# A selective-scan kernel: a third product buffer, an earlier gate copy, and u's projection and the front spread over a batch's blocks in another way

## What is computed

```python
x = einsum('ed,bld->bel', in_proj_w, hidden_states)            # 1024 channels
xc = causal depthwise convolution of x, 4 taps
u = silu(xc + conv_b)
x_dbl = einsum('ke,bel->bkl', x_proj_w, u)                     # dt (32), B (16), C (16)
delta = softplus(dt_proj_w @ dt_lo + dt_proj_b);  A = -exp(A_log)
state = state * exp(d_t * A) + (d_t * u_t) * B_t               # 16 states for each channel
y_t = sum over n of state * C_t
y = (y + D * u) * silu(z)                                      # z = layernorm(x)
x = x + y
n = layernorm(x)
x = x + n @ W_base.T + b_base + top-2-gated low-rank experts of n
```

## Time and profile before

| | us |
|---|---|
| median of 3 runs | 2175.45 |
| lowest and highest | 2169.37, 2175.68 |
| profiled execution | 2179.93 |
| its span in the trace | 2178.1 |
| before the first scan | 91.1 |
| E0 to E31, from first scan to last scan's end | 1910.2 |
| behind the last scan | 176.8 |

### The profile page before, as it was taken

The page is one execution under the profiler, slowest core; times in us unless marked ns, Lnnn a source line. Parts: engine busy times, 40 slices in busy tenths (PEclk is TensorE's granted clock), DMA queues, the critical chain, the costliest instruction groups (busy, mean ns, idle before and its releaser), DMA issues.

```text
span 2178.1 us, 23728 instructions
## 1 busy us (share of the span) xinstructions
PE 1812.5 (83%) x7992; PEld 1097.9 (50%) x7992; DVE 1789.7 (82%) x1430; ACT 1255.9 (58%) x1701; POOL 1774.2 (81%) x798
## 2 busy tenths in 40 slices
PE   9877777777778888888888888888888888878999
PEld 3344444454455555555555555555555545555554
DVE  3589898888898899987999999987999999997111
ACT  3355555456566666655766666655766666663432
POOL 0389888889898998988999998988999999997300
PEclk9777787778779999998999999998999999999999
DMA  4665555576755656685666665685755556665300
GB/s 157 242 233 189 188 180 185 180 247 245 236 189 183 208 205 210 224 282 212 221 207 210 214 206 205 222 277 176 240 195 202 201 205 213 213 213 193 136 29 34
DMA packets 157977, 435.88 MB, mean 200 GB/s; under 512 B 14528, under 2 KB 47552, under 8 KB 157728
## 3 DMA queue, kind: packets, MB, share of 16 engines
q1 hardware_dynamic: 157856, 434.37, 58.1%
HBM read 383.46 MB, written 50.86 MB: 199 GB/s over the span
## 4 chain that ended last, share of the span: by engine, by line
DVE 33%; PE 30%; POOL 15%; issue 13%; ACT 6%; DMA 4%; SPq 0%; DVEq 0%; POOLq 0%; ACTq 0%
DVE state L1051 21%; POOL prod L1188 10%; DVE row L1036 9%; PE bank_a L548 7%; PE y_ps L492 6%; POOL drive_rows L1181 3%; PE bank_b L443 3%; DVE conv L1028 3%; PE bank_b L548 3%; PE row L570 3%; DMA xrow<-in_x 2%; ACT decay L807 2%; PE bank_b L472 2%; PE row L486 1%; PE bank_b L452 1%
## 5 line engine op out<-in xcount | busy, mean ns | idle before, releaser
L1188 POOL TENSOR_TENSOR prod<-state,c_rows 128x1024 f32<-128x1024 f32 x512 | 1201.2, 2359 | 163.4 <-PE y_ps L492 132.9
L1051 DVE TENSOR_TENSOR_SCAN state<-decay,row 128x1024 f32<-128x1024 f32 x332 | 758.0, 2283 | 9.5 <-POOL prod L1188 2.4
L492 PEld LDWEIGHTS y_ps<-ident,prod 128*128 128x128 f32 x4096 | 516.7, 152 | 343.3 <-issue 173.9
L492 PE MATMUL y_ps<-ident,prod 128*128 128x128 f32 x4096 | 596.9, 294 | 82.8 <-POOL prod L1188 81.2
L1036 DVE TENSOR_TENSOR row<-du,row 128x1024 f32<-128x1024 f32 x332 | 402.1, 1211 | 105.5 <-PE row L486 102.9
L1051 DVE TENSOR_TENSOR_SCAN state<-row,drive_rows 128x1024 f32<-128x1024 f32 x180 | 409.8, 2277 | 21.8 <-POOL drive_rows L1181 21.5
L1181 POOL TENSOR_TENSOR drive_rows<-du,b_rows 128x1024 f32<-128x1024 f32 x180 | 425.4, 2364 | 2.0 <-DMA b_rows<-bc_d 2.0
L807 ACT ACTIVATE row<-delta,a 128x1024 f32<-128x1024 f32 x180 | 201.0, 1117 | 389.2 <-DVE state L1051 388.8
L548 PE MATMUL bank_a<-w_o,xnT 128*128 128x512 f32 x816 | 400.2, 622 | 30.1 <-DVE x L1098 30.1
L807 ACT ACTIVATE decay<-delta,a 128x1024 f32<-128x1024 f32 x332 | 372.2, 1135 | 0.1
L486 PE MATMUL row<-parts,sel 96*128 96x512 bf16 x664 | 221.7, 418 | 119.4 <-DVE state L1051 114.4
(11 more groups left out here) (131 smaller groups left out, 1653.1 us busy)
## 6 DMA issues: line engine op xcount, KB each, us to landing
c_rows<-bc_d SPq DMA_DIRECT2D x512, 512.0 KB, 4.3
xrow<-in_x SPq DMA_DIRECT2D x32, 512.0 KB, 6.6
skip<-u_d SPq DMA_DIRECT2D x32, 512.0 KB, 5.8
yy_d<-yy SPq DMA_DIRECT2D x32, 512.0 KB, 6.2
b_rows<-bc_d SPq DMA_DIRECT2D x24, 512.0 KB, 6.0
u_d<-conv SPq DMA_DIRECT2D x24, 512.0 KB, 5.3
ctx<-u_d SPq DMA_DIRECT2D x48, 256.0 KB, 5.9
x<-in_x SPq DMA_DIRECT2D x24, 512.0 KB, 5.9
```

The costliest lines, as they stand in the source:

```text
L492: last = nc.tensor.matmul(y_ps[:, i * P:(i + 1) * P], source[:, i * P:(i + 1) * P], ident[:, :], start=(first and i % (H // P) == 0), stop ...
L1051: nc.vector.tensor_tensor_scan(state[:, q % STATES, :], factor, term, 0.0, ALU.mult, ALU.add).then_inc(scan_done, 1)
L1188: nc.gpsimd.tensor_tensor(prod[:, q % PRODS, :], state[:, q % STATES, :], c_rows[:, q % RING, :], ALU.mult).then_inc(prod_ready, 1)
```

## The change

PRODS goes from 2 to 3 and RING from 5 to 4, the same memory. The front's table has one form for all batches: blocks 0 to 5 of a batch make 3, 3, 2, 3, 3, 2 halves of the next batch and blocks 6 and 7 none (before, batches 1 and 2 had 3, 2, 2, 3, 2, 2, 0 and block 7 began the batch after next with two). Where it is spread out, the first half's pieces move from sections 0 to 3 to sections 2, 3, 4, 4, and its conv and taps from 5 to 6. turn_gate stands in sections 2 and 3 and take_gate in 3 and 4, but in a batch's last block in 4, 5 and 5, 6. reduce_u of the first half is in sections 5 to 8 of block 6, two matmuls each, and that of the second half in sections 0 to 3 of block 7; the copies, the split, dt_half, the gate's sums, store_bc, load_b, load_us and load_ctx move behind it. The diff:

```diff
--- before.py
+++ after.py
@@ -24,7 +24,7 @@
 LATE = 9
 FIRST_SPLITS = 6
 FIRST_TAIL = NBLK - LATE
-RING, DECAYS, STATES, PRODS, DRIVES = 5, 4, 3, 2, 2
+RING, DECAYS, STATES, PRODS, DRIVES = 4, 4, 3, 3, 2
 
 
 
@@ -32,19 +32,15 @@
 DECAY_AT[12] = DECAY_AT[13] = 10
 
 
-EARLY = [[(0, 0), (0, 1), (1, 0)], [(1, 1), (2, 0), (2, 1)], [(3, 0), (3, 1)], [(4, 0), (4, 1), (5, 0)],
+FRONT = [[(0, 0), (0, 1), (1, 0)], [(1, 1), (2, 0), (2, 1)], [(3, 0), (3, 1)], [(4, 0), (4, 1), (5, 0)],
          [(5, 1), (6, 0), (6, 1)], [(7, 0), (7, 1)], [], []]
-LATER = [[(1, 0), (1, 1), (2, 0)], [(2, 1), (3, 0)], [(3, 1), (4, 0)], [(4, 1), (5, 0), (5, 1)],
-         [(6, 0), (6, 1)], [(7, 0), (7, 1)], [], [(0, 0), (0, 1)]]
 
 
 def front_halves():
     table = []
     for E in range(NBLK):
         b, r = E // NE, E % NE
-        ahead = b + (2 if r == NE - 1 else 1)
-        rows = EARLY if b == 0 and r < NE - 1 else LATER
-        table.append([(ahead * NE + c, h) for c, h in rows[r]] if ahead < B else [])
+        table.append([((b + 1) * NE + c, h) for c, h in FRONT[r]] if b + 1 < B else [])
     return table
 
 
@@ -52,7 +48,7 @@
 HALF_INDEX = {u: i for i, u in enumerate(u for row in HALVES for u in row)}
 
 
-SPREAD_OUT = (((0, 1, 2, 3), (5, 6, 7, 8), (9, 10, 11, 12)), (5, 10, 14), (5, 10, 15))
+SPREAD_OUT = (((2, 3, 4, 4), (5, 6, 7, 8), (9, 10, 11, 12)), (6, 10, 14), (6, 10, 15))
 IN_ONE_GO = (((5,), (8,), (12,)), (7, 10, 14), (7, 10, 15))
 
 
@@ -353,10 +349,11 @@
                 load_c(E * DS + m + RING - 1)
                 last = r == NE - 1 and b + 1 < B
                 if last:
-                    if m == 0:
+                    if m == 4:
                         store_bc(b + 1)
-                    if m - 1 in B_ROWS:
-                        load_b(b + 1, B_ROWS.index(m - 1))
+                    for i, n in enumerate(B_ROWS):
+                        if m == max(n + 1, 6 + i):
+                            load_b(b + 1, i)
                 if m == 2 and j >= 1:
                     store_half(j - 1, 1)
                 if m == 3:
@@ -382,10 +379,10 @@
                     if m == 0:
                         for s in range(NE):
                             load_us(b + 1, s)
-                    if m in (6, 7, 8):
-                        for s in range(NE + 3 * (m - 6), min(NE + 3 * (m - 6) + 3, 2 * NE)):
+                    if 7 <= m <= 10:
+                        for s in range(NE + 2 * (m - 7), NE + 2 * (m - 7) + 2):
                             load_us(b + 1, s)
-                if r == NE - 1 and m == 0 and b + 2 < B:
+                if r == NE - 1 and m == 5 and b + 2 < B:
                     for k in range(NK):
                         load_ctx(b + 2, k)
                 if E == NBLK - 1 and m == 6:
@@ -602,10 +599,17 @@
                 if ((q + 1) // DS, (q + 1) % DS) in D_INDEX:
                     spread((q + 1) // DS, (q + 1) % DS)
 
-                if m < 2 and E + 1 < NBLK:
+                last = r == NE - 1 and b + 1 < B
+                if last and m < 4:
+                    reduce_u(b + 1, 1, range(2 * m, 2 * m + 2))
+                if last and m in (4, 5):
+                    turn_gate(E, m - 4)
+                if last and m in (6, 7):
+                    dt_half(E + 1, m - 6)
+                if not last and m < 2 and E + 1 < NBLK:
                     dt_half(E + 1, m)
-                if m in (2, 4):
-                    turn_gate(E, m // 2 - 1)
+                if not last and m in (2, 3):
+                    turn_gate(E, m - 2)
 
                 if dense and m in (2, 3):
                     turn(j, m - 2, beside, True)
@@ -616,9 +620,9 @@
 
                 for i, at in enumerate(front_plan(E)[0]):
                     if m in at and len(HALVES[E]) > i and m < 9:
-                        project(E, i, [at.index(m)] if len(at) > 1 else range(NK))
-                if r == NE - 2 and b + 1 < B and 5 <= m <= 7:
-                    reduce_u(b + 1, 0, range(3 * (m - 5), min(3 * (m - 5) + 3, NE)))
+                        project(E, i, [k for k in range(NK) if at[k % len(at)] == m])
+                if r == NE - 2 and b + 1 < B and 5 <= m <= 8:
+                    reduce_u(b + 1, 0, range(2 * (m - 5), 2 * (m - 5) + 2))
 
                 if dense:
                     if m in (6, 7, 9, 10):
@@ -630,9 +634,7 @@
                         experts(j, 0, beside)
                 for i, at in enumerate(front_plan(E)[0]):
                     if m in at and len(HALVES[E]) > i and m >= 9:
-                        project(E, i, [at.index(m)] if len(at) > 1 else range(NK))
-                if r == NE - 2 and b + 1 < B and 12 <= m <= 14:
-                    reduce_u(b + 1, 1, range(3 * (m - 12), min(3 * (m - 12) + 3, NE)))
+                        project(E, i, [k for k in range(NK) if at[k % len(at)] == m])
                 if dense:
                     if m >= 13:
                         product(j, 1, range(3 * (m - 13), min(3 * (m - 13) + 3, NE)), beside, True)
@@ -919,35 +921,37 @@
                         make_decay(*step)
                 if m == 0:
                     scale_skip(E)
-                if m in (1, 2) and E + 1 < NBLK:
+                last = r == NE - 1 and b + 1 < B
+                if not last and m in (1, 2) and E + 1 < NBLK:
                     take_v(E + 1, m - 1)
+                if last and m == 4:
+                    take_xd(b + 1, 1)
+                    split_first(b + 1)
                 if dense and m in (3, 4):
                     take_turned(j, m - 3, beside, True)
-                if m in (3, 5):
-                    take_gate(E, (m - 3) // 2)
+                if not last and m in (3, 4):
+                    take_gate(E, m - 3)
+                if last and m in (5, 6):
+                    take_gate(E, m - 5)
+                if last and m in (7, 8):
+                    take_v(E + 1, m - 7)
+                if last and m == 7:
+                    split_second(b + 1)
                 if dense and m == 5:
                     take_routing(j, beside)
                 if dense and m == 7:
                     exp_gap(j)
                 if E + 1 < NBLK:
-                    if m == 7:
+                    if m == (8 if last else 7):
                         gate_sum(E + 1)
-                    if m == 8:
+                    if m == (9 if last else 8):
                         gate_squares(E + 1)
                     if m == 9:
                         gate_scale(E + 1)
-                if r == NE - 2 and b + 1 < B:
-                    if m == 8:
-                        take_xd(b + 1, 0)
-                    if m == 15:
-                        take_xd(b + 1, 1)
-                if r == NE - 1 and b + 1 < B:
-                    if m == 0:
-                        split_first(b + 1)
-                    if m == 3:
-                        split_second(b + 1)
-                    if m == 6:
-                        split_third(b + 1)
+                if r == NE - 2 and b + 1 < B and m == 9:
+                    take_xd(b + 1, 0)
+                if last and m == 10:
+                    split_third(b + 1)
 
                 if E + 1 < NBLK:
                     if m == 10:
@@ -1136,6 +1140,8 @@
                         dve.wait_ge(xd_copied, 2 * (b + 1) + 1)
                     elif len(HALVES[E]) > 1:
                         dve.wait_ge(conv_done, HALF_INDEX[HALVES[E][1]] + 1)
+                    elif r == NE - 1 and b + 1 < B:
+                        dve.wait_ge(v_copied, 2 * (E + 1))
                     else:
                         dve.wait_ge(gate_copied, 2 * E + 2)
                     gates(j, beside)
@@ -1218,8 +1224,8 @@
                 product(E * DS + m)
                 if j >= -1 and m in (7, 10):
                     add_x(j + 1, (7, 10).index(m))
-                if r == NE - 1 and b + 1 < B and m in (1, 4):
-                    split_rest_of(b + 1, m == 1)
+                if r == NE - 1 and b + 1 < B and m in (6, 8):
+                    split_rest_of(b + 1, m == 6)
                 if m == 12 and E + 1 < NBLK:
                     make_du(E + 1)
```

## The result

| | before | after |
|---|---|---|
| median, us | 2175.56 | 2099.48 |
| lowest and highest | 2169.37, 2183.69 | 2095.79, 2104.84 |
| profiled execution | 2179.93 | 2104.84 |
| before the first scan | 91.1 | 92.6 |
| blocks E0 to E31 | 1910.2 | 1835.7 |

A forecast was written before the change was run, and what follows sets the result against it. No engine is full; TensorE, working in order, hands its waits on to VectorE and GpSimd. Terms summed to -66.1 us, giving 2113.8 from the profiled execution, 2109 as median; range 2080 to 2150 us.

The forecast's parts named there:

- gate and third halves, E9 to E13, E16 to E21: Dense blocks: 16 us gained by copying the gate earlier, 5 us lost to third halves in four blocks.
- E14, E22: Block 6 of two batches: moving eight matmuls out takes each from 68.2 to 57.7 us, 21 us together.
- the gate's 1.6 us in ten blocks: Ten dense blocks: copying the gate a section earlier removes TensorE's bank wait, 16 us in all.
- the start's 3.4 us: First block: c row 3 now stands behind w_o's 4 MB load, so product 4 starts 3.4 us later.
- rival C: Crowded sections 3 to 5: c rows land late and GpSimd waits, 96 us slower, 2205 us; chance 0.07.
- Rival A: TensorE itself is the bound, so only moved matmuls and third halves count: 20 us gained, 2155 us; chance 0.16.
- the third product buffer: Product q waits for add-up q-3; worth lies in other parts and in batch 3, where 5 us were taken.
- the pieces of sections 0 to 2: Six spread-out blocks: moving two project pieces to sections 2 to 4 gains 3.5 us a block, 21 us.
- the third halves (+5 us in the sum): Blocks 1 and 4 of batches 1 and 2: an extra half each costs 9 us on VectorE, gives 4 back.
- the 2.7 us of idle time that I gave it from E19: First batch's block 7: GpSimd's work plus this idle time makes 57.5 us against 61.2, a gain of 3.7 us.
- the 2.9 us that the prediction added to E14 and E22: Sections 12 to 14 lose their filling, so TensorE's clock drops as in E10: 2.9 us a block.
- the split of x_dbl: Block 7, moved to sections 4 to 10: ScalarE's wait there was taken as 0, bounds 0 and 5 us.

The follow-up runs named there:

- E31: Not a run: the last of the kernel's blocks, E0 to E31, which take 1910.2 us before the change and 1835.7 after.
- E8: Not a run: a block of the kernel where the front is spread out, grouped with E1 to E5 in the prediction.
- E15: Not a run: a block 7 of a batch in the kernel, 60.4 us in the changed kernel's rerun.
- E23: Not a run: a block 7 of a batch in the kernel, 59.4 us in the changed kernel's rerun.
- the two runs of the gate: Changed kernel with the gate's old sections, 2121.2 us; kernel before with only turn_gate in 2 and 3 and take_gate in 3 and 4, 2156.5 us.
- the second profile: The changed kernel, unaltered, run again beside later variants: 2097.6 us.
- E18: Not a run: a dense block of the kernel with two halves, 59.3 us in the changed kernel's rerun.
- E10: Not a run: a dense block of the kernel with two halves, 56.1 us in the changed kernel's rerun.
- the three left-out parts: Changed kernel with two product buffers and ring of five, 2117.1 us; with the gate's old sections, 2121.2; with first-half pieces back in sections 0 to 3, 2107.3.
- their own run: Changed kernel with w_o loaded in eight pieces, one in section 9 of each of eight blocks, and w_ra later in section 12: 2098.5 us.
- the run of all four: Changed kernel with large weights loaded later, residual rows loaded earlier, product y's last pieces in section 12 and exponentials ahead of the split: 2069.4 us.
- the early rows: Changed kernel with xrow loaded in section 4 ahead of the y rows instead of section 5, except in a batch's last block: 2089.7 us.
- E24: Not a run: a block of the kernel, 57.9 and 56.0 us in the two profiles of the changed kernel.
- the added matmuls: Changed kernel with four unused matmuls behind the expert multiplies in sixteen dense blocks with fewer than three halves: 2115.2 us.
- the moved ones: Changed kernel with product y's last two pieces moved from section 10 to 12 in sixteen blocks with fewer than three halves: 2083.4 us.

## Why the prediction was right, step by step

The total fell 76 us where 66 were forecast: inside the range and close, though part of that is luck, since two terms were off in opposite directions.

| term | forecast | blocks of the profile |
|---|---|---|
| batch 3 | -5 | -7.0 |
| gate and third halves, E9 to E13, E16 to E21 | -11 | -13.7 |
| E1 to E5, E8 | -21 | -17.2 |
| E14, E22 | -21 | -23.7 |
| E6; E7 | -3.5; -3.7 | -4.9; -7.2 |
| E15, E23 | -4.3 | -4.2 |
| E0 | +3.4 | +3.4 |
| before the first scan; behind the last | 0 | +1.5; -2.1 |

**What was right.** The reading that TensorE's waits are handed on, so that GpSimd's 132.9 us and VectorE's 68.7 us are not the engines' own; that E14 and E22 are worth the most in single blocks, and that a moved projection takes them to 58 us or less (58.1; 54.6); the gate's 1.6 us in ten blocks (the two runs of the gate give 19 and 22 us for 16); the idle time that remains (94 us forecast, 90.1 measured); the start's 3.4 us (see below); and VectorE's wait for spread rows, 23.1 us where more than 40 would have spoken against the forecast. The c rows, rival C, did nothing outside E0: 0.4 us in all. Rival A falls with E19: it idled 2.7 us beside its busier engine and idles 1.4 now, at 53.5 us of TensorE in 58.6.

**What was mis-sized.** First, the third product buffer. The step "Alone it does not move a spread, so its worth lies in the parts below" is right as to spread rows (102.9 to 92.2 us), and wrong as to the worth: alone it gave 27 us, 17.8 of them in E1 to E8, and 17.6 within the change; the term had 5. GpSimd's wait for the add-up was on the path there, not only idle time beside it. Second, the pieces of sections 0 to 2. The term took all that E1 to E5 and E8 could lose, 21 us; in these blocks 7.8 of the measured 17.2 came back without the pieces and 4.7 without the buffer, and the buffer alone took 14.8 from them: the two stand for the same time in part. The working read the two waits of E2 and took them both for the pieces' doing; with two causes for one wait, the sum is right and the attribution is not. In E2 itself the pieces are worth nothing. Gated_y's waits up to E8 were to fall below 10 us and fell from 21.6 to 16.2.

The table's second row hides that the two batches differ. E9 to E13 fell from 305.2 to 290.0 us, while E16 to E21 went from 358.6 to 359.9 (353.7 in the second profile), though the gate alone took them to 348.4 in the kernel before. What took back there what the gate gives is open. In E18 and E21 the clock fell, as shown above, which is some 3 us in each against E10 and E13; the third halves (+5 us in the sum) were not tried alone.

Third, E7: the 2.7 us of idle time that I gave it from E19 was 0.4, and GpSimd had 53.6 us of work where the working left 54.8. Fourth, the start: the wait for product 3's row ends at 117.35, not 115.4, and product 4 starts at 121.95, 5.2 us later than before. But 1.5 of these are the later first scan (92.6 against 91.1), and from the block's start product 4 is 3.7 us later where 3.4 was forecast, so this term was right by its mechanism. Only the wait is longer, 12.6 us and not 8: GpSimd, which had waited 2.9 us for an add-up ahead of it, comes to it earlier. Fifth, the 2.9 us that the prediction added to E14 and E22 for the lower clock. In the first profile VectorE waits 2.1 us at step 15 in E14 and not at all in E22, where the clock held; in the second it waits 0.5 us and not at all. What the prediction took as a price of every such block is one that some of them pay. Last, where I put the split of x_dbl at nothing, "since the decays for DVE's next steps are issued before it", I looked at the decays and forgot exp_gap, which stands behind it in the same section: 2.5 us in E15 and 3.4 in E23, inside the bounds of 0 to 5 given for each.

**What stays open.** How much of the 29 us beyond the three left-out parts is the halves' new table, apart from u's projection, was not tried. That E0's 8 us do not show in the total of their own run, and at most in half in the run of all four, has no cause that the runs show. By which waits the early rows gain most of their 8 to 10 us is open too.

## What to carry to other kernels

With engines that wait in order, a wait's price is not seen on the engine that waits: follow it to the engine that was late, and look there for a wait of its own (a bank that another engine has not copied, a product, a row that has not landed). A buffer more is worth trying by itself before the rest is planned around it, for it relieves both sides of a loop. An idle stretch ahead of work that others wait for is to be filled with work that is moved, not with work that is added: the idle time and the lower clock do not vanish, they move to where nobody waits. Count such an effect over all the blocks that have it, for a single block can be picked to show either outcome. A load issued one section earlier was worth 8 to 10 us here, and is cheap to try.

## What the runs showed of the hardware

**The clock.** In E24 of the changed kernel TensorE idled 4.0 us, from 1529 to 1533, at a granted 1.00 (2.4 GHz), and the 8 us behind it show 0.57, most of them at the lower level (1.2 GHz), though TensorE was busy throughout; from 1541 on it is 1.00 again. The price falls on what stands behind the idle time, 4.38 us for six records that take 2.74 us in the stretch after. The Trainium skill's "TensorE: Matmul & The Clock Gate", section Why this matters for your kernels, advises against idle stretches between bursts of matmuls. The trace agrees in part: behind the same 2.81 us of idle time the clock fell in E18 and E21 (5.49 us for six records) and not in E10 and E13 (2.84). As to the time, the added matmuls cost 16 us and the moved ones gained 14.

**ScalarE's table loads.** They take 1.28 us each, and the next activation starts as soon as they end:

```profile
1527.86 1.28 ACT L678 ACT_TABLE_LOAD   x1
1529.15 1.06 ACT L732 ACTIVATE delta<-delta 128x1024 f32<-128x1024 f32 x1
```

The Trainium skill's "ScalarE: Activation LUTs", section What ACT_TABLE_LOAD costs, gives the same 1.28 us and adds a drain of about 1.4 us to each switch. Here no such time is seen: the decays ahead end 0.02 us before the load (1525.67 and 2.17 us). The trace decides: a switch costs 1.3 us on this list.

**One load behind another.** A c row that stood behind a load of 4 MB kept GpSimd waiting 12.55 us; with that load issued later the longest wait for a c row is 0.6 us.
